# Memory attention and second norm in 20 steps of one tile, with the normalization on GpSimd

## The reference, cut to what matters

```python
scores = einsum('bsd,bmd->bsm', ln(x), ctx) / sqrt(512)   # 128 memory tokens per image
scores = where(mask[:, None, :], scores, -1e30)
readout = einsum('bsm,bmd->bsd', softmax(scores), ctx)
x = x + where(any(mask, -1), readout, 0)
h = ln(x)
queries = (h @ W_q)        # first product of the fourth layer; the MLP reads h too
```

## Time and profile before

| | us |
|---|---|
| median of 3 runs | 2090.32 |
| profiled execution, its own time | 2089.45 |
| its span in the trace | 2087.7 |
| busy in the span: TensorE | 1836.0 (88%) |
| VectorE | 1205.9 (58%) |
| ScalarE | 870.9 (42%) |
| GpSimd | 822.2 (39%) |

### The profile page before, as it was taken

One profiled execution on the slowest core, in us unless ns is written; L12 is line 12 of the kernel. 1 busy time (PEld: TensorE's weight loads), 2 busy tenths in 40 slices (PEclk: granted clock), 3 DMA queues, 4 the chain that ended last, 5 costly groups with the idle time before them and its releaser, 6 DMA issues.

```text
span 2087.7 us, 39748 instructions
## 1 busy us (share of the span) xinstructions
PE 1836.0 (88%) x13025; PEld 1086.0 (52%) x13029; DVE 1205.9 (58%) x2650; ACT 870.9 (42%) x1790; POOL 822.2 (39%) x691
## 2 busy tenths in 40 slices
PE   1586998998989489999999999997569989999998
PEld 1335666666655256666666666664444434444443
DVE  7854777777766433333333333332785677777776
ACT  3435877777666134334444344442232222212211
POOL 3102336555565533444344444442001344554542
PEclk7698999999999789999999999999689999999999
DMA  5314557776765256666676676453210345565554
GB/s 195 111 61 125 165 177 170 176 181 186 157 148 127 54 168 163 142 141 163 142 166 142 145 170 124 94 87 60 92 45 12 114 143 186 169 210 202 189 181 164
DMA packets 149136, 294.82 MB, mean 141 GB/s; under 512 B 40432, under 2 KB 77936, under 8 KB 144688
## 3 DMA queue, kind: packets, MB, share of 16 engines
q1 hardware_dynamic: 97968, 157.48, 26.5%
q0 software_dynamic: 46368, 126.29, 24.8%
q10 hardware_dynamic: 4608, 8.52, 1.3%
HBM read 426.00 MB, written 78.33 MB: 242 GB/s over the span
## 4 chain that ended last, share of the span: by engine, by line
PE 66%; issue 8%; POOL 8%; DVE 8%; ACT 5%; DMA 4%; another core or an unknown queue 1%; ACTq 0%; SPq 0%; POOLq 0%; DVEq 0%
PE bank L205 19%; PE bank L207 19%; PE bank L206 19%; POOL expert_tokens L2114 3%; PE bank L999 2%; DMA x_sum<-x,work_arena 2%; DVE work_arena L1466 2%; PE bank L1026 2%; ACT xt_arena L1246 1%; POOL work_arena L2091 1%; DVE work_arena L168 1%; DVE ln_st L155 1%; POOL xt_arena L2100 1%; DMA x<-token_rows,work_arena 1%; POOL xt_arena L2110 1%
## 5 line engine op out<-in xcount | busy, mean ns | idle before, releaser
L205 PE MATMUL bank<-work_arena,xt_arena 128*128 (+1 forms) x1285 | 417.9, 327 | 6.9 <-DVE xt_arena L174 3.3
L206 PE MATMUL bank<-work_arena,xt_arena 128*128 (+1 forms) x1285 | 417.7, 327 | 0.0
L207 PE MATMUL bank<-work_arena,xt_arena 128*128 (+1 forms) x1285 | 417.7, 327 | 0.0
L2187 POOL DMA_INDIRECT x_sum<-x,work_arena x111 | 176.3, 1589 | 400.3 <-DMA x_sum<-x,work_arena 176.7
L205 PE MATMUL bank<-work_arena 128*128 128x512 f16 (+1 forms) x680 | 260.7, 386 | 48.5 <-DVE work_arena L1466 20.0
L1940 DVE TENSOR_TENSOR xt_arena<-xt_arena,bank 128x352 f32<-128x352 f32 x111 | 57.8, 521 | 372.4 <-PE bank L207 347.7
L206 PE MATMUL bank<-work_arena 128*128 128x512 f16 (+1 forms) x680 | 261.1, 386 | 0.0
L207 PE MATMUL bank<-work_arena 128*128 128x512 f16 (+1 forms) x680 | 260.4, 385 | 0.0
L205 PE MATMUL bank<-xt_arena,work_arena 128*128 128x512 f16 (+1 forms) x560 | 212.7, 380 | 1.0 <-DVE xt_arena L174 1.0
L206 PE MATMUL bank<-xt_arena,work_arena 128*128 128x512 f16 (+1 forms) x560 | 212.3, 379 | 0.0
L207 PE MATMUL bank<-xt_arena,work_arena 128*128 128x512 f16 (+1 forms) x560 | 212.2, 379 | 0.0
(11 more groups left out here) (254 smaller groups left out, 3823.1 us busy)
## 6 DMA issues: line engine op xcount, KB each, us to landing
work_arena<-expert_w SPq DMA_DIRECT2D x111, 1408.0 KB
work_arena<-expert_w SPq DMA_DIRECT2D x111, 768.0 KB
work_arena<-in_moe_w SPq DMA_DIRECT2D x64, 352.0 KB
expert_w<-work_arena SPq DMA_DIRECT2D x86, 176.0 KB
work_arena<-in_moe_w SPq DMA_DIRECT2D x48, 256.0 KB
work_arena<-in_mlp_w SPq DMA_DIRECT2D x8, 1536.0 KB
work_arena<-in_head_w SPq DMA_DIRECT2D x16, 512.0 KB, 3.5
expert_w<-work_arena SPq DMA_DIRECT2D x64, 128.0 KB
```

Source lines behind the costliest of these rows:

```text
L205: pe.matmul(o, a_hi, b_hi, start=start, stop=False)
L206: pe.matmul(o, a_hi, b_lo, start=False, stop=False)
L207: return pe.matmul(o, a_lo, b_hi, start=False, stop=stop)
L2187: pool.indirect_dma_start(out=xacc[:, :], out_offset=bass.IndirectOffsetOnAxis(ap=rid[:, i:i + 1], axis=0), in_=ysb[:, b % YB, :], in_offs ...
```

## The change

- The stage runs in 20 steps (`END_STEPS` = 16 + 4) of one tile. Step n holds norm 2 of tile n (statistics, GpSimd) and of tile n - 1 (transposes, high, low), scores and maximum of tile n - 1, exponential, turn and readout of tile n - 2, add, statistics and GpSimd part of norm 3 for tile n - 3, and transposes, high and low of norm 3 for tile n - 4.
- GpSimd does the normalization: power, then a tensor_scalar (subtract, multiply) of 128x512 fp32 into `xn`.
- The readout is one fp32 product of `mpt` (fp32, 128x128) and `mem` (fp32, as loaded). So `ctx` isn't split any more, and VectorE loses half of `split_memory`.
- The maximum is scaled on ScalarE in place of VectorE.
- Norm 2 turns through bank 4, norm 3 through bank 5, scores and turned probabilities share bank 6, the readout uses bank 7, queries banks 0, 1, 2 and 4.
- Queries of groups 0, 1 and 2 are made in steps 8, 12 and 16, their high and low parts one step later; the first weights are split in steps 15, 16 and 17.
- ScalarE copies the key weights ahead of its loop.
- SP loads the first four tiles of x one by one, then three loads of four.

The diff, cut to its core:

```diff
+        END_STEPS = B + 4
+        QUERIES_AT = {4 * t + 8: t for t in range(NB - 1)}
+        WEIGHTS_AT = {15 + piece: piece for piece in range(3)}
 # SP
+            for b in range(LS):
+                sp.dma_start(x[:, b, :], xacc[b * P:(b + 1) * P, :]).then_inc(x_in[b], 16)
+            for q in range(1, LN_IT):
                 sp.dma_start(x[:, q * LS:(q + 1) * LS, :], ...).then_inc(x_in[q], 16)
 # TensorE
+            def memory_readout(b):
+                pe.wait_ge(mem_load[1], 16 * B)
+                pe.wait_ge(mem_pt, b + 1)
+                if b > 0:
+                    pe.wait_ge(mem_added, b)
+                pe.matmul(bank[7][:, :], mpt[:, b % 2, :], mem[b // LS][:, b % LS, :], start=True,
+                          stop=True).then_inc(mem_read, 1)
+            for n in range(END_STEPS):
+                if in_end(n - 1):
+                    end_turn(2, n - 1)
+                if in_end(n - 2):
+                    memory_turn(n - 2)
+                if in_end(n - 4):
+                    end_turn(3, n - 4)
+                if in_end(n - 2):
+                    memory_readout(n - 2)
+                if in_end(n - 1):
+                    memory_scores(n - 1)
+                if n in QUERIES_AT:
+                    pe.wait_ge(pk_s, 2)
+                    key_queries(QUERIES_AT[n])
+            key_queries(NB - 1)
+            pe.wait_ge(pk_ql, NB - 1)
             mlp_up(0)
 # ScalarE
-            ln_high(act, LN_AT[2, 0], 0)
             act.wait_ge(consts_in, 96 + 16)
             act.activation(kw_hi, kw32, ACT.Copy, scale=WS).then_inc(pk_s, 1)
+            for n in range(END_STEPS):
+                if in_end(n - 2):
+                    memory_exps(n - 2)
+                if in_end(n - 1):
+                    end_high(2, n - 1)
+                if in_end(n - 2):
+                    memory_copy(n - 2)
+                if in_end(n - 4):
+                    end_high(3, n - 4)
+                if n - 1 in QUERIES_AT:
+                    queries_high(QUERIES_AT[n - 1])
+                if n in WEIGHTS_AT:
+                    mlp_split(0, WEIGHTS_AT[n])
+            queries_high(NB - 1)
 # VectorE
+            for n in range(END_STEPS):
+                if in_end(n - 3):
+                    memory_add(n - 3)
+                    end_stats(3, n - 3)
+                if n == 2:
                     dve.wait_ge(pk_s, 1)
                     lo_of(kw_lo, kw32, WS, kw_hi).then_inc(pk_s, 1)
+                if in_end(n - 1):
+                    end_low(2, n - 1)
+                if in_end(n - 4):
+                    end_low(3, n - 4)
+                if n < B:
+                    dve.wait_ge(x_in[n if n < LS else n // LS], 32 if n < LS else 48)
+                    end_stats(2, n)
+                if in_end(n - 2):
+                    memory_factor(n - 2)
+                if in_end(n - 1):
+                    memory_max(n - 1)
+                if n - 1 in QUERIES_AT:
+                    queries_low(QUERIES_AT[n - 1])
+                if n in WEIGHTS_AT:
+                    mlp_split(0, WEIGHTS_AT[n])
+            queries_low(NB - 1)
 # GpSimd
+            def end_normalize(which, b):
+                i = norm_at(which, b)
+                pool.wait_ge(ln_stat, 2 * NT + 3 * i + 3)
+                pool.tensor_tensor(ln_rs[:, b, :], ln_ve[:, b, :], neg_half[:, 0, :], ALU.pow).then_inc(ln_rstd, 1)
+                pool.wait_ge(ln_rstd, LN_IT + i + 1)
+                pool.tensor_scalar(xn[:, b, :], x[:, b, :], ln_mv[:, b, 0:1], ln_rs[:, b, :], ALU.subtract,
+                                   ALU.mult).then_inc(ln_norm, 1)
+            for n in range(END_STEPS):
+                if in_end(n - 3):
+                    end_normalize(3, n - 3)
+                if n < B:
+                    end_normalize(2, n)
```

More of the change, by code:

```diff
@@ new lines, in memory_scores @@
+            def memory_scores(b):
+                g, i = divmod(b, LS)
+                pe.wait_ge(ln_lo, low_at(2, b) + 1)
+                if b >= 2:
+                    pe.wait_ge(mem_exp, b - 1)
+                o = bank[6][:, b % 2 * P:(b % 2 + 1) * P]
+                pe.matmul(o, idbf[:, :], mm_bias[:, b, :], start=True, stop=False)
+                for c in range(DC):
+                    m = mm3(pe, o, cols_of(xt_hi, b)[:, c, :], cols_of(xt_lo, b)[:, c, :],
+                            memT_hi[g][:, c, i * P:(i + 1) * P], memT_lo[g][:, c, i * P:(i + 1) * P], start=False,
+                            stop=(c == DC - 1))
+                m.then_inc(mem_scored, 1)
@@ L1984, in memory_low, with end_stats @@
-            def memory_low(g):
-                dve.wait_ge(mem_pt_hi, g + 1)
-                dve.tensor_tensor(mpt_lo.rearrange("p a b -> p (a b)"), bank[5][:, :],
-                                  mpt_hi.rearrange("p a b -> p (a b)"), ALU.subtract).then_inc(mem_pt_lo, 1)
-                dve.wait_ge(mem_sums, 2 * g + 2)
-            def memory_add(g):
-                for i in range(LS):
-                    b, k = g * LS + i, i % 2
-                    dve.wait_ge(mem_read, b + 1)
-                    dve.scalar_tensor_tensor(out=x[:, b, :], in0=bank[6 + k][:, :], scalar=mfac[:, i:i + 1],
-                                             in1=x[:, b, :], op0=ALU.mult, op1=ALU.add).then_inc(mem_added, 1)
+            def end_stats(which, b):
+                i = 2 * NT + 3 * norm_at(which, b)
+                dve.bn_stats(ln_st[:, which, :], x[:, b, :]).then_inc(ln_stat, 1)
+                dve.wait_ge(ln_stat, i + 1)
+                dve.bn_aggr(ln_mv[:, b, :], ln_st[:, which, :]).then_inc(ln_stat, 1)
+                dve.wait_ge(ln_stat, i + 2)
+                dve.tensor_scalar(ln_ve[:, b, :], ln_mv[:, b, 1:2], EPS, None, ALU.add).then_inc(ln_stat, 1)
@@ new lines, in end_low, with memory_max @@
+            def end_low(which, b):
+                dve.wait_ge(ln_hi, turn_at(which, b) + 1)
+                dve.tensor_tensor(cols_of(xt_lo, b), bank[2 + which][:, :].rearrange("p (a b) -> p a b", a=DC),
+                                  cols_of(xt_hi, b), ALU.subtract).then_inc(ln_lo, 1)
+            def memory_max(b):
+                dve.wait_ge(mem_scored, b + 1)
+                dve.tensor_reduce(mmax[:, b % 2:b % 2 + 1], bank[6][:, b % 2 * P:(b % 2 + 1) * P], AX.X, ALU.max,
+                                  negate=True).then_inc(mem_max, 1)
```

253 lines of the change are left out of this document (100 added, 153 removed).

## The result

| | before | after |
|---|---|---|
| median of 4 runs each | 2091.15 | 2129.06 us (2121.13 to 2130.56) |
| profiled execution, its own time | 2089.45 | 2129.29 |
| its span | 2087.7 | 2127.3 |
| TensorE busy | 1836.0 | 1851.3 |
| VectorE busy | 1205.9 | 1186.9 |

The ratio of the times is 1.0164, 95% interval 1.0138 to 1.0191: slower by over 0.5%. (The two medians alone would give 1.0181; the ratios in this document are those on record, which differ a little from the quotient of the medians.) The forecast was 2128.0, range 2103 to 2147, with 0.88 on slower.

A forecast was written before the change was run, and what follows sets the result against it. The norm-2 chain, 6.82 us a tile, was taken to bound the stage; with start, additions and tail its end moves from 1564.2 to 1602.1. 2089.45 + 37.9 + 0.87 = 2128.2 us, range 2103 to 2147.

The forecast's parts named there:

- the chain of norm 2: Copies, low part, statistics, power, normalize and transposes, once round per tile: 4.89 us + t a step.
- t: GpSimd's normalize of one tile, 128x512 fp32 with two operations: taken as 1.93 us, low end 1.04, high end 2.3.
- Rivals B: Same chain, but t near tensor_tensor's 1.04 us: 2112 us in all; chance 0.25.
- C: Rival: not slower, GpSimd normalizing at VectorE's pace, 0.48 us a tile: 2095 us; chance 0.12.
- The step: One tile's pass through the new pipeline: 6.82 us, steps 1 to 3 0.85 less, against 6.20 an image before.
- The port wait: VectorE's two-SBUF-input factor product waits about 1.0 us for GpSimd's power each step, hidden with 0.4 us of slack left.
- Rival D: Factor product waits for both power and normalize; step about 8.2 us, +16.6 us, 2145 us; chance 0.13.
- the sum: Start, steps, additions and tail put the last key queries near 1602.1 instead of 1564.2: +37.9 us.
- The start: First high copy waits behind the key weights' landing and copy, until 1474.7; some 5 us lost.
- the additions: Extras on the steps up to tile 15: kw_lo +0.9, low clock +3.2, key queries +2 us.
- The tail: Steps 15 to 19 on VectorE, weight splits waiting for GpSimd and delaying adds: +20 us to the last key queries.
- Costed at nothing: Work taken as hidden: maximum, exponential, readout beside GpSimd's normalize; removed half of split_memory; SP's waits; groups' removed low part.

The follow-up runs named there:

- e2: Kernel after with the norm-2 statistics put ahead of the low parts in VectorE's step; stage 125.59 us, 1.0100 of before.
- e3: Kernel after with GpSimd normalizing each tile twice for norm 2; stage 173.58 us, one run, 2165.18 us beside 2090.4 of before.
- e11: Kernel after with both reorderings, e1 and e2 together, GpSimd still normalizing; stage 118.64 us, 1.0066 of before.
- e1: Kernel after with ScalarE's key-weight copy moved to step 4 and VectorE's kw_lo to step 5; stage 128.05 us, 1.0112 of before.
- e9: e7 with the splits of the first MLP weights moved to steps 18 and 19, behind the last adds; stage 101.07 us, 0.9977 of before.
- e7: Kernel after with key weights copied in step 4, norm-2 statistics ahead of the low parts, and ScalarE normalizing; stage 106.42 us, 1.0011 of before.
- e4: Kernel after with the fp32 readout product issued twice into the same bank; stage 139.50 us, one run, 2131.86 us beside 2090.4 of before.
- e12: e9 with epsilon and the mean's factor -1 moved from VectorE to GpSimd, readout factor left on VectorE; stage 97.17 us, 0.9960 of before.

## Why the prediction was right, and where it was not

- **The bound and the direction: right.** It predicted that the order on VectorE ties tile to tile, and that the chain of norm 2 with t in it sets the step. The chain of after shows it link by link, e2 cuts it, e3 stretches it by 2.24 us for each normalize added. One link is drawn otherwise than the prediction had it: the low part of norm 2 follows its own copy at once, and both low parts stand in the chain (1.98 us from copy to statistics), where the prediction went through ScalarE's two other copies (2.07). Rivals B (t 1.04) and C (t 0.48) fall with t = 2.08.
- **The step: the main terms off, against each other.** t was taken as 1.93, measured 2.08 in nearly all 32 instances. The power with its wait was taken as 1.10, measured 0.56 + 0.10 = 0.67. Forecast 6.82, measured 6.56 in a plain step. The second error was avoidable: the value came from the groups of four in the earlier trace rows (128x4, 1.01), although the row above it in the same group is a power of 128x1 with 0.57, the very form of the change. The right form gives 6.39 with the t of the prediction and 6.54 with the measured one. The rest nearly cancels: transposes with hand-over 0.69 (forecast 0.53), statistics 1.09 (1.19), copies and low parts 1.98 (2.07), and 0.05 for GpSimd's start and end. That the sum came within 4% is in part luck.
- **The port wait: wrong in its place.** The factor product was to wait 1.0 us; it took 0.16 to 0.18 beside the power. Rival D rested on it and falls. Beside GpSimd's normalize such a product of 128x1 took up to 0.41 in e2 and 0.61 in e11. `kw_lo` is where two-input work met GpSimd's normalize, and there GpSimd was held up, not VectorE: 2.85 in place of 2.08, beside 0.95, what `kw_lo` took in the kernel before too. That is the +0.9 of the sum, measured 0.77.

```profile
1491.11 0.56 POOL L2246 TENSOR_TENSOR ln_rs<-ln_ve,neg_half 128x1 f32<-128x1 f32 x1 [3.62 <-DVE ln_ve L2023]
1491.13 0.18 DVE L2040 TENSOR_TENSOR work_arena<-work_arena 128x1 f32<-128x1 f32 x1
1484.64 2.85 POOL L2248 TENSOR_SCALAR work_arena<-x,ln_mv,ln_rs 128x512 f32<-128x512 f32 x1
1484.75 0.95 DVE L1513 SCALAR_TENSOR_TENSOR work_arena<-work_arena 128x768 f16<-128x768 f32 x1
```

  The Trainium skill, "GPSIMD Engine Reference", § 8 Key points, says that the two engines share SBUF interfaces; the second pair of rows agrees with it; in the first, product and power went on side by side.
- **The start: the mechanism right, its size not.** First copy 15.5 us behind the first load, measured 16.97. The loss was put at 5 us because tile 0's own way was taken to end 10.4 us behind the first load (1469.6); e1 shows 8.9, and the key weights were there 16.2 us behind the first load (1480.83), where the old landing time had given 14.8. The loss is 8.1 us in the trace, and e1's first copy comes 8.1 us earlier.
- **First to last norm-2 copy**: forecast 105.8 us (1474.7 to 1580.5), measured 102.5. The step was 0.26 too long, over 12 steps 3.1 us: this is the difference, and the additions came out right as a sum, 5.9 against 6.1. The trace shows their parts. The first three steps took 20.3 in place of 17.9 plus the 0.9 for `kw_lo`. Of the twelve others, five took 6.56 and six 6.97 to 7.02, about 0.4 more with transposes at the low clock: 2.6 us in all, forecast 3.2. The step behind the queries of step 8 took 0.85 more, the one behind step 12's nothing; forecast 2.
- **The tail**: forecast 20.0, measured 18.2, but only in part for the reason given. The prediction had VectorE's list, with each split blocked by GpSimd and then ahead of an add. The splits took 1.43, 1.22 and 1.21 us (alone 1.22), and only the last stands in the chain that ends the stage. Ahead of it the chain runs through TensorE: the transposes, the readout of tile 14 at low clock (1.88 us, priced at nothing), the scores, and the twelve products of the queries of step 16 (2.8 us), for which the sum has no term. They hold up the next high copy (1591.74), and with it VectorE. The second split ended 5.8 us behind the last norm-2 copy where 6.7 was forecast, but it had waited for the scores (the maximum at 1588.44), not for GpSimd: a nearly right time from a wrong wait. e9 shows splits in the chain for e7, where the steps are shorter; no run isolates them in the kernel after.

```profile
1585.14 1.88 PE bank L1153 x2
1588.40 0.38 PE bank L199
1591.74 0.61 ACT xt_arena L1448
1593.85 1.21 DVE work_arena L1513
1595.06 0.67 DVE x L2046
```

- **Costed at nothing**: the fp32 readout. That holds in the plain steps (e4), not in the tail. The part behind the stage grew by 1.5, where 1.6 for queries at low clock was forecast.
- **Not forecast**: 5.4 us ahead of the stage. The stage and what follows grew by 34.2, against 37.9 forecast. The medians agree to about 1 us only because this too large sum and the displacement cancel, which is luck; by its working the prediction was off by 3.7 us, within its range. The ratio on record, 1.0164, is 34.3 us, what the stage and the part behind it grew by.
- **t by the page**: the same page of the Trainium skill, § 4.1 Engine selection, has one-input work "roughly line-rate", which is 0.43 us by its clock, an estimate. The trace has 2.08: the row of 7.13 us for 128x2048 was the better guide, as forecast.

## What to carry to other kernels

Moving work to an idle engine helps only if it leaves the chain: here an engine with 39% load took over a step that costs it four times as much (2.08 against 0.54 us), in the middle of the round trip of every tile. Before such a move write down the round trip of one step with each engine's order in it; the cheapest repair was not a faster instruction but an order (statistics ahead of the low parts, the weight copy out of the way of the first tile). And price an instruction by the row of its own shape, even where a row with more columns has the same name.

## What the hardware showed

- GpSimd's two-operation tensor_scalar, fp32: 2.08 us at 128x512 and 7.13 at 128x2048, so, as an estimate that takes both for the same kind of work, 3.29 ns an element and 0.40 fixed. The prediction had 3.39 and 0.19.
- Where VectorE's work with two SBUF inputs met GpSimd's normalize, one of the two was held up, and which one went by who began first, give or take 0.12 us. VectorE first, or no more than 0.12 us behind: GpSimd's instruction took 2.85 (kernel after, e3, e4; e11, where VectorE was first) or 3.14 us (e4, a split) in place of 2.08, VectorE's kept its time. VectorE 0.17 to 0.47 us later: GpSimd's kept its 2.08 and VectorE's was drawn out, by 0.45 (e11, 0.17 later), 0.38 (e3, 0.24), 0.22 (kernel after, 0.40, the rows below) and 0.16 (e1, 0.47). Each time the two add up to 0.62 or 0.63 (0.59 to 0.60 for the one-column products of e2 and e11), so GpSimd's instruction kept VectorE off for about its first 0.6 us only; a split that began 1.15 us behind it (e2) took its 1.21. Why it is 0.6 no run shows. The four VectorE normalizes of the earlier trace rows are another instruction beside another, 7.13 us long, and are not explained by this.

```profile
1580.83 2.08 POOL L2248 TENSOR_SCALAR work_arena<-x,ln_mv,ln_rs 128x512 f32<-128x512 f32 x1
1581.23 1.43 DVE L1513 SCALAR_TENSOR_TENSOR work_arena<-work_arena 128x1024 f16<-128x1024 f32 x1
```

- The granted clock over the whole stage was 0.74 in before, 0.71 in after, 0.67 in e3 (longer steps), 0.84 in e7 and 0.89 in e12 (shorter ones), and 0.83 in e4, where TensorE had more to do in plain steps of the same length as in after. So a slower chain was paid for twice here, with the transposes of a tile at 1.12 us (1521.32 in after) and 0.66 at full clock:

```profile
1521.32 1.12 PE bank L1125 x4
1528.75 0.66 PE bank L1125 x4
```
